# Last weight piece, modulation table and bias ring: another order of the opening work in a four-layer transformer stack

## The reference

```python
x = rotate(x, theta[b], phi[b])                      # pairs of features, by an angle of the sample
x = LN(x + gelu(x @ Wi[e] + bi[e]) @ Wo[e] + bo[e])  # one of 8 experts, 256 -> 1024 -> 256
x = LN(x + branch[c](x)) * gamma + beta              # one of three small networks
emb = silu(sin_emb(timestep)) @ W_ada + b_ada        # 32 x 512: scale and shift of each sample
scale, shift = split(emb)
x = LN(x) * (1 + scale) + shift
x = x + softmax(q k' / 4 + bias[b], masked) v @ Wo   # 16 heads, bias is 16 x 256 x 256 per sample
x = x + gelu2(LN(x) @ W1 + b1) @ W2 + b2
```

## Time and profile before

| | |
|---|---|
| median of 3 runs | 2216.45 us (2213.16 to 2218.63) |
| the profiled execution, its time | 2213.16 us |
| its span in the trace | 2211.4 us |
| TensorE busy | 2014.0 us, 91% |
| VectorE busy | 1566.3 us, 71% |
| ScalarE busy | 1312.3 us, 59% |
| transfers issued by SyncE | 344.37 MB, 51.1% of 16 engines |

### The profile page before, as it was taken

How to read it: one execution, slowest core, us unless ns; L and a number is a source line. 1 busy time by engine, 2 the same in 40 slices (tenths; PEclk the granted TensorE clock), 3 DMA queues, 4 the chain that set the end, 5 groups by cost and what they waited for, 6 DMA issues and landing times.

```text
span 2211.4 us, 43730 instructions
## 1 busy us (share of the span) xinstructions
PE 2014.0 (91%) x14735; PEld 1734.5 (78%) x14735; DVE 1566.3 (71%) x5410; ACT 1312.3 (59%) x2084; POOL 123.5 (6%) x268
## 2 busy tenths in 40 slices
PE   4789999999999999999999999999999999999887
PEld 3678887788878878878788787878787788877776
DVE  5567777776677677777767777767677767776864
ACT  3456566566666666656665666666656576656433
POOL 1000000000000000000000000000000000000000
PEclk9899999999999999999999999999999999999989
DMA  6455454554554445554545455545555545554440
GB/s 233 145 173 177 148 151 155 169 156 147 166 170 151 154 144 173 170 167 149 175 116 179 153 160 169 168 142 176 159 169 169 173 128 170 171 163 143 136 143 25
DMA packets 217606, 347.52 MB, mean 157 GB/s; under 512 B 29139, under 2 KB 115443, under 8 KB 217364
## 3 DMA queue, kind: packets, MB, share of 16 engines
q1 hardware_dynamic: 217364, 344.37, 51.1%
HBM read 285.51 MB, written 58.79 MB: 156 GB/s over the span
## 4 chain that ended last, share of the span: by engine, by line
PE 63%; DVE 12%; DMA 8%; issue 6%; SPq 6%; ACT 4%; DVEq 0%; POOL 0%; ACTq 0%; POOLq 0%
PE pD L452 42%; PE pX L667 8%; DMA out<-res 7%; PE pS L452 7%; SPq L293 5%; DVE x_scores L1158 4%; PE pC L452 3%; PE pD L457 2%; DVE x_scores L944 2%; ACT gelu_out L764 2%; DVE res L947 2%; ACT hid L764 1%; PE pC L687 1%; DVE res L941 1%; DVE hid L941 1%
## 5 line engine op out<-in xcount | busy, mean ns | idle before, releaser
L1158 DVE CUSTOM_DVE_ANT_0 x_scores<-pS,bias_ring 128x256 f32<-128x256 f32 x1024 | 391.1, 419 | 215.6 <-PE pS L452 201.5
L764 ACT ACT_TABLE_LOAD x345 | 442.6, 1283 | 34.6 <-PE pD L452 27.5
L764 ACT ACTIVATE probs<-pX 128x512 f32<-128x512 f32 x512 | 304.8, 595 | 262.6 <-PE pX L667 257.6
L667 PE MATMUL pX<-ident,x_scores 128*128 128x128 f32 x2048 | 324.8, 282 | 52.7 <-DVE x_scores L944 49.7
L667 PEld LDWEIGHTS pX<-ident,x_scores 128*128 128x128 f32 x2048 | 235.0, 143 | 124.3 <-DVE x_scores L944 92.9
L944 DVE TENSOR_SCALAR x_scores<-x_scores,row_max 128x256 f32<-128x256 f32 x1024 | 315.6, 351 | 18.3
L452 PE MATMUL pS<-k_stack,q_stack 96*128 96x256 f32 x1024 | 305.8, 381 | 0.0
L452 PE MATMUL pD<-x,raw 128*128 128x256 f32 x1024 | 245.9, 383 | 1.8 <-ACT gelu_out L764 1.0
L452 PE MATMUL pD<-raw,gelu_out 128*128 128x256 f32 x1024 | 241.6, 379 | 0.0
L452 PEld LDWEIGHTS pS<-k_stack,q_stack 96*128 96x128 f32 x1024 | 199.3, 195 | 22.7
L452 PEld LDWEIGHTS pD<-raw,gelu_out 128*128 128x128 f32 x1024 | 189.6, 190 | 23.7 <-issue 0.4
(11 more groups left out here) (152 smaller groups left out, 3617.4 us busy)
## 6 DMA issues: line engine op xcount, KB each, us to landing
bias_ring<-in_fside SPq DMA_DIRECT2D x512, 256.0 KB, 3.3
raw<-in_experts SPq DMA_DIRECT2D x128, 512.0 KB, 6.3
q_spill<-hid SPq DMA_DIRECT2D x96, 256.0 KB, 3.3
k_spill<-hid SPq DMA_DIRECT2D x96, 256.0 KB, 3.3
q_stack<-q_spill SPq DMA_DIRECT2D x128, 192.0 KB, 3.3
k_stack<-k_spill SPq DMA_DIRECT2D x64, 384.0 KB, 5.4
x_nat<-in_x SPq DMA_DIRECT2D x32, 256.0 KB, 7.7
norm<-in_expert_rows SPq DMA_DIRECT2D x32, 256.0 KB, 7.6
```

Source lines behind the costliest of these rows:

```text
L667: last = e.transpose(pX[:, k, t * P:(t + 1) * P], x_scores[:, u % NX, t, k * P:(k + 1) * P], ident[:, :])
L764: return e.activation(o, i, func, bias=bias, scale=scale)
L1158: e.tensor_tensor_reduce(x_scores[:, xn, t, :], pS[:, t, :], bias_ring[:, n, t, :], 1.0, -3.4e38, ALU.add, ALU.max, row_max[:, xn, t:t + 1 ...
```

## The change

Three moves, all in the once-only stream; no operation is added or dropped.

- SyncE: piece 10 is loaded straight behind piece 9, ahead of `load_x(1)` and `load_norm1(1)`. The four bias loads stand ahead of the store of the modulation table and `load_norm3(0)`.
- TensorE: the modulation products stand one step later, behind the transposes of y1 and ahead of `branch_in`.
- VectorE: the modulation result is written behind piece 4, ahead of the low part of the branch.

```diff
@@ SyncE, weights()
-                for pieces in ((6,), (7, 8), (9,)):
+                for pieces in ((6,), (7, 8), (9, 10)):
                     for i in pieces:
                         piece(i)
                     yield
+                e.wait_ge(sem["dve_w"], runs_before(NSTAGE * PIECE))
+                for u in range(NBIAS):
+                    load_bias(u)
                 e.wait_ge(sem["dve_mod"], 1)
                 load(mod_rows, mod_made, "dma_mod")
                 e.wait_ge(sem["dma_mod"], 16)
                 load_norm3(0)
-                e.wait_ge(sem["dve_w"], runs_before(NSTAGE * PIECE))
-                for u in range(NBIAS):
-                    load_bias(u)
-                piece(10)
                 yield
@@ TensorE, weights()
-                for _ in range(9):
+                for _ in range(10):
                     yield
@@ VectorE, weights()
                 yield
                 yield
+                yield
+                piece(4)
                 e.wait_ge(sem["pe_mod"], 1)
                 step(ts(mod_made[:, 0:H], pD[0:NB, TAIL, 0, :], 1.0, ALU.add))
                 step(e.tensor_copy(mod_made[:, H:2 * H], pD[0:NB, TAIL, 1, :]), "dve_mod")
-                yield
-                piece(4)
                 yield
```

## The result

The changed kernel took 2228.55 us, median of 7 runs (2219.24 to 2230.53). The kernel before took 2213.88 beside it (7 runs, 2211.26 to 2218.63). The ratio is 1.0054, with a 95% interval of 1.0036 to 1.0073: slower by 0.54%. Forecast were 2227.5 us and 0.50%.

A forecast was written before the change was run, and what follows sets the result against it. TensorE is busy 2014.0 of 2211.4 us, but the serial opening chain was taken to decide: 8.6 us for late `norm3` plus 2.5 for the products, 11.1 on 2216.45, gives 2227.5 us, 0.50% slower; range 2221 to 2234.

The forecast's parts named there:

- SyncE's order: Opening, SyncE: it stops at early piece 10 for VectorE's piece 6, holding back the loads and store behind; `norm3` 8.6 us later.
- spare times: Opening: time between landing and use before the change, 13.5 us for x(1) and 11.4 for `norm3`; both used up.
- The sum behind piece 10: Opening, SyncE: issues 3.0, store 4.6 and `norm3` load 3.0 us put `norm3` at T + 10.6, between T + 9.9 and T + 15.2.
- T: End of VectorE's piece 6, which SyncE's piece 10 waits for; 55.9 us if nothing else moves.
- The store: Modulation table's store, queued behind seven 256 KB transfers at 322 GB/s: lands 4.6 us after issue, bounds 3.9 to 6.5.
- the load of `norm3`: Load following the store on SyncE: lands 3.0 us later as before, 5.7 at most.
- The products: Modulation products on TensorE, moved in front of the branch products, begin at half clock: cost 2.5 us, bounds 0 to 6.
- The bias loads and VectorE's result: Opening: bias loads' 1.76 us issue and 1 MB queue already counted; VectorE's modulation result costs 0, or 0.8 if not covered.
- Reaches the end whole: Whole run: an opening delay shifts everything behind it by one constant, unless a later wait does not move with it.
- The sum: Whole run: total delay of 8.6 + 2.5 = 11.1 us, with bounds 7.9 and 19.2.
- absorbed later: Rival, chance 0.13: the stretch 92.4 to 100 gives back up to 4.7 us, leaving 6.4, within 0.3%.

The follow-up runs named there:

- e1: Kernel before with only piece 10 loaded straight behind piece 9; ratio to the kernel before 1.0025 (1.0009 to 1.0042).
- e3: Changed kernel with piece 10 put back to the end of SyncE's step, other moves kept; ratio to the kernel before 1.0007 (0.9993 to 1.0020).
- e12: Repeat of e1, the kernel before with piece 10 alone early; 2229.16 us, ratio to the kernel before 1.0029 (1.0009 to 1.0049).
- e2: Kernel before with only the moves on TensorE and VectorE, SyncE as before; ratio to the kernel before 1.0008 (0.9994 to 1.0023).
- e7: Changed kernel with 20 products of zeros in TensorE's idle time ahead of the y1 transposes; ratio to the kernel before 1.0038 (1.0024 to 1.0051).
- e4: Changed kernel with piece 10 behind load_x(1) and load_norm1(1), ahead of bias loads and store; ratio to the kernel before 1.0041 (1.0025 to 1.0058).
- e8: Kernel before with q of sample 0 ahead of sample 1's first expert product and two low parts made later; ratio 0.9999 (0.9984 to 1.0015).
- e11: Repeat of e6, piece 10 early and bias loads held until norm3 landed; 2225.82 us, ratio to the kernel before 1.0015 (0.9998 to 1.0032).
- e6: Against e1, bias loads held back until norm3 has landed; ratio to the kernel before 1.0005 (0.9994 to 1.0016).
- e5: The changed kernel run again without further change; ratio to the kernel before 1.0047 (1.0028 to 1.0065).

## Why the prediction was right

*SyncE's order.* Right, and shown by one line put in and taken out: e1 has the 8.2 us with nothing else changed, e3 loses them again with everything else changed. SyncE stopped at piece 10 for 22.8 us. Both spare times that the forecast had read, 13.5 us for x(1) and 11.4 for `norm3`, were used up, and `norm3` was last, as forecast.

*The sum behind piece 10.* Forecast T + 10.6, measured 12.42. The burst took 3.58 us to issue (3.0 forecast), with 0.75 us from piece 10 to x(1) alone. The store took 5.8 (4.6 forecast), and the load of `norm3` 3.0 (3.0). The store was the mis-sized term: I reckoned with seven transfers at 322 GB/s and got 4.7, and took 4.6, but the burst moved at 232 GB/s. Store and load were inside their bounds; the issue had none. Less the 2.0 us that the step came behind T before, it came 10.4 us later, not 8.6. By the runs, these 10.4 us are 8.2 of piece 10 alone (7.5 in e12) and 2.2 of the bias move on top (up to 4.3).

The Trainium skill (DMA: Bandwidth & Descriptors, "Anatomy of one DMA") would have 2.0 us plus bytes over 436 GB/s. That fit is per DMA on GpSimd's path, and has no term for other transfers in flight. For a store of 64 KB it gives an estimate of 2.15, against 1.6 for the lone store of e2, 3.1 to 3.7 behind three loads and 5.8 to 6.5 behind seven. For 256 KB it gives 2.6. Piece 10 took 2.6, which agrees; `norm3` took 3.0 to 3.5 with nothing beside it, and 4.7 to 4.9 with four loads beside it.

*The products.* Forecast 2.5 us (0 to 6), measured 1.8 by the first traces (18.99 - 17.16), 1.3 against the other two of before (17.73). The bounds were right for their reason: e7 moves the branch's activation by 2.3 us with the clock alone, and e4's slow stretch costs 2 to 3 us more. The path between them was right too: the products began at the half clock, and the branch products behind them found it raised (0.28 us each, 0.42 before). The Trainium skill (TensorE: Matmul & The Clock Gate, "Why this matters for your kernels") says that idle gaps bring the clock down; the trace agrees, 0.50 behind 4.98 us of idling in the changed kernel and 1.00 in e7 where the gap was filled.

*The bias loads and VectorE's result.* The move of the bias loads was priced with the store's queue, which is right only together with piece 10 (e3: nothing). The modulation result cost nothing visible: e2 has both moves and 1.2 to 1.8 us in all.

*Reaches the end whole.* The sum was 11.1, the opening's measured delay 11.9 to 12.6 us, the span's 12.4, the median's 14.7; the ratio, 0.54%, is 12.0. The two errors are of opposite sign, 1.8 too little behind piece 10 and 0.7 too much ahead of it. That 2227.5 lies within 1.1 us of the measured 2228.55 is luck: the sum was added to 2216.45, and the kernel before took 2213.88 in the comparison.

The forecast's rival "absorbed later" named a place, the stretch from 92.4 to 100. There nothing came back. The same stretch 12.2 us later in the changed kernel is as long and as idle (2.94 of 7.6 us busy on TensorE, as in the earlier trace rows):

```profile
104.60:112.20 7.60, 2.94 (x19) 2.49 (x20) 4.05 (x11) 5.21 (x7) 0.00 (x0) 0.95 0.44 149
```

SyncE's load of x of sample 3 says the same, first before and then changed:

```profile
136.66 0.35 SPq L293 DMA_DIRECT2D x_nat<-in_x  x1
148.94 0.35 SPq L293 DMA_DIRECT2D x_nat<-in_x  x1
```

Is a late opening whole at the end in every run? In e1, e4 to e8, e11 and e12 the measured loss is smaller than the late opening, by some 1 to 5 us each (lateness of the maxima against the mean of before, less the ratio times 2220 us): e6 and e11 are late by 6 to 8 and lose 1 to 3. But their traces keep the lateness as far as it can be read. At the load of x of sample 6, some 330 us behind the transposes, it is 5.6 us in e6, 8.4 in e11 and 8.5 to 14.8 in the others with piece 10 early; none is more than 1 us less late there than at its first maxima. Further on the traces of before drift apart by themselves, 9.6 us at sample 15, and from the first maxima to the end they took 2124 to 2131 us, the eleven others 2124 to 2139. So whether a part of a late opening is given back later stays open, and why e6 and e11 lost so little with it.

## What to carry to other kernels

On an engine that issues all the loads in a fixed order, a load's price is not its own lateness but that of all that stands behind its wait. Ask of each wait that is moved forward when it ends, and which later load has the least slack against that time; here 6 us of harmless waiting at the end of a step became 23 us at its head. Then put what the chain needs (a small store and the load that follows it) ahead of bulk that has slack, and keep bulk from going out right beside it: holding the bias loads back brought the `res` step 1.0 to 1.5 us closer to piece 10 (e6 and e11 against e1 and e12), though the time does not tell these apart.

## What the runs showed of the hardware

- A 64 KB store landed 1.6 us behind its issue with nothing else in flight (e2), and later with each 256 KB load issued right ahead of it: 3.1 to 3.7 us behind three (e1, e6, e11, e12), 4.1 behind four (e3), 4.5 behind five (e4), 5.8 to 6.5 behind seven (the changed kernel, e5, e7).
- The 256 KB load of `norm3` took 3.0 to 3.5 us alone and 4.7 to 4.9 with four loads issued right behind it, so transfers issued later slow an earlier one that has not landed.
- After 5.0 us of idling TensorE ran 0.50 of its clock. With zeros multiplied in that gap it ran at 1.00 and the same two products took 1.91 in place of 3.56 us; but the next burst, 2.6 us of idling later, then fell to the half clock.
- How long the half clock lasts differs between traces with the same TensorE program: the 18 parts behind the transposes took 6.12 us in the changed kernel, 6.33 in e3 and 8.27 in e4.
